# The deformable gather as one stream, its row coordinates all sent by DMA in 8-KB pieces

## The chip, the cores and the metric

The kernel runs on one core of one Trainium2 chip. The metric is the device time of one launch in microseconds, the median of the runs. Everything is float32 at the interfaces; some matmuls read their operands as float32r or bf16.

## The reference, cut to what matters

The network has four layers. The first is a gated selective scan, the second a mixture of experts, the third a bottleneck of three deformable convolutions, the fourth a wide 1x1 mix. The change touches the third layer only: the function `_deform` there, called three times, on 8 images of 256, 64 and 64 channels of 32x32 pixels.

```python
def _deform(x, ow, ob):                      # x: (8, C, 32, 32)
    off = _conv(x, ow, 1) + ob               # two offsets for each channel and pixel
    py = jnp.clip(yy + off[:, :, 0], 0.0, H - 1)
    px = jnp.clip(xx + off[:, :, 1], 0.0, W - 1)
    y0, x0 = floor(py), floor(px); y1, x1 = min(y0 + 1, H - 1), min(x0 + 1, W - 1)
    wy, wx = py - y0, px - x0
    v00, v01, v10, v11 = g(y0, x0), g(y0, x1), g(y1, x0), g(y1, x1)   # g: gather inside the channel
    return v00*(1-wy)*(1-wx) + v01*(1-wy)*wx + v10*wy*(1-wx) + v11*wy*wx
```

Each output pixel of each channel is thus a bilinear sample of that channel's own 32x32 image at a position of its own.

## The kernel before

**The gather without a gather.** The kernel does no indexed access. `build_offsets_1` and `build_middle` write to HBM, for each channel, the image as steps (`dense`: differences of neighbours in both directions), the positions split in a high and a low part (`coords`), and the row positions whole (`whole`). `build_gather` then computes, for 32 rows i and a channel, kw = min(max(py + 1 - i, 0), 1), the same for the columns (vw), and sums dense[i, j] * kw[i] * vw[j] over i and j. The step form of the image makes this the bilinear sample.

**Sets, quads and units.** 128 channels are a set. There are 16 sets in the first gather (g1, 256 channels), 4 in the second (g2) and 4 in the third (g3). A set has 2 halves of 512 pixels (`HALF`) with 8 quads each, so 16 quads; a quad is 16 channels, laid out as 4 groups r of 32 partitions by 4 units c. All three gathers together have 384 quads. Four sets make one turn of a loop (`nc.Fori(0, blocks // SETS)`): g1 has 4 turns, g2 and g3 one each, 6 turns of 64 quads. A turn is a block of its own: its engines start together, all semaphores wait for the end, and nothing of the next turn is loaded before.

**One quad, by engine.** SP (`send_rows`) waits until the row buffer is free (`rows` has SB = 3 slots) and sends, for each r, the row positions of 3 channels (SENT = 3) from `whole` to 32 partitions, each partition the same bytes: 4 DMAs of 3 x 2 KB x 32. VectorE (`relu`) adds 1 - i and takes the maximum with 0 over those 3 units at once, into `kw`. The fourth unit (OWN = 1) comes another way: TensorE spreads its coordinate with a 128x128 selection matmul (`spread_step`, task "k") into a ring of 3 PSUM banks, ScalarE evacuates it. The four column units come by the same ring (tasks "v"), so 5 spread matmuls and 5 evacuations a quad. GpSimd clamps the four `kw` units at 1. TensorE sums over rows (`rows_step`, 16 small 32x32 matmuls into 4 PSUM banks that are not doubled), VectorE multiplies the result by `vw` out of these banks (`weigh`, two instructions of 128x1024), TensorE sums over columns (`fold_step`, 4 matmuls).

**What sets the order.** TensorE takes in turn n: rows_step(n), three spreads, fold_step(n-1), the other spreads. VectorE takes weigh(n) and then relu(n+2). rows_step(n) waits for weigh(n-1), because it writes the banks that weigh reads; weigh(n) waits for rows_step(n). SP issues in program order on one queue: the rows of quad 0, all loads of the first set, the rows of quads 1 and 2, all loads of the other three sets, and only then the rows of quad 3 and on. The loads of a set (`load_set`) are 4 DMAs of 512 KB for `coord` (both directions, high and low: 128 partitions, L1351) and 4 of 128 KB for `img` (L1357), which pick 128-byte pieces out of `dense`. Results go out every 8 quads by one DMA of 256 KB (`store`, L1363).

## Time and profile before

| | |
|---|---|
| median of 3 runs | 5976.52 us (5972.13 to 5980.63) |
| the profiled execution | 5969.8 us, of it the span 5968.1 us |
| TensorE busy | 81% of the span, mean granted clock 0.887 |
| VectorE, ScalarE, GpSimd busy | 60%, 31%, 25% |
| DMA | 558.13 MB in 377577 packets; 37.7% of 16 engines |
| the gathers with the two middle stages between them | about 3610 to 5781 us of the span |
| row positions sent | 1536 DMAs of 192 KB |

The page divides the span into 40 slices. The last 16 of them are this part of the kernel; there DMA stands at 8 and 9 tenths in most slices, and in most slices before at 0 or 1. The shares of the whole span therefore say little about it: the part has to be read by windows. In the rows below, a line of the windows view gives each engine's busy time and, behind PEclk, the granted TensorE clock as a part of 2.4 GHz (0.50 is 1.2 GHz), the mean busy share of the 16 DMA engines (it passes 1 where packets of one engine overlap) and the rate.

### The profile page before, as it was taken

Reading aid. Unit: us, or ns where it says so; the run is one execution under the profiler, and the core shown is the slowest. Engines: PE = TensorE matmul, PEld = TensorE weight load, DVE = VectorE, ACT = ScalarE, POOL = GpSimd, SP = SyncE. Lnnn points to the kernel's source line nnn. Section 1 sums busy time; section 2 is a strip of 40 time slices with the busy share of each in tenths; the row PEclk is TensorE's granted clock in tenths of the full one; section 3 lists DMA queues with packets and bytes.
Section 4 is the critical chain, followed back from the end, with each engine's and each line's share of the span. In section 5 each row is a group of like instructions: output and inputs, shape, how many; then the busy total and the mean of one; then the engine's idle time right before and its main releaser. Section 6 shows DMA issues by size and latency. Waiting matters only on the chain. (4 is left out here: it accounts for less than half of the span.)

```text
span 5968.1 us, 82574 instructions
## 1 busy us (share of the span) xinstructions
PE 4860.9 (81%) x30592; PEld 2689.8 (45%) x30592; DVE 3608.7 (60%) x4317; ACT 1857.1 (31%) x2899; POOL 1478.1 (25%) x1828
## 2 busy tenths in 40 slices
PE   4787887876999799979989994959596983985886
PEld 2333333324777677757767771313131332332222
DVE  6888888875666566652212223848484873863764
ACT  2222222202222122220000003848484751751660
POOL 0222222220000000011101002636363651642540
PEclk7888888867999899989999996979797996997988
DMA  1000000001000000011111119989898968978962
GB/s 30 15 20 17 21 22 21 15 21 65 15 15 8 22 15 15 8 61 74 43 71 74 53 67 193 217 180 218 178 220 181 217 171 183 218 145 143 221 178 91
DMA packets 377577, 558.13 MB, mean 94 GB/s; under 512 B 167464, under 2 KB 169064, under 8 KB 376264
## 3 DMA queue, kind: packets, MB, share of 16 engines
q1 hardware_dynamic: 377160, 552.64, 37.7%
q8 instruction: 253, 4.15, 0.3%
q14 instruction: 164, 1.34, 0.1%
HBM read 439.27 MB, written 113.25 MB: 93 GB/s over the span
## 5 line engine op out<-in xcount | busy, mean ns | idle before, releaser
L1415 POOL TENSOR_SCALAR g_kw<-g_kw 128x512 f32<-128x512 f32 x1536 | 960.8, 650 | 936.7 <-ACT g_kw L1401 637.1
L1401 ACT ACTIVATE g_vw<-ps,l_index 128x512 f32<-128x512 f32 x1536 | 971.0, 686 | 520.4 <-PE ps L1457 520.1
L1434 DVE SCALAR_TENSOR_TENSOR g_prod<-g_vw,ps 128x1024 f32<-128x1024 f32 x768 | 903.3, 1218 | 213.0 <-PE ps L1472 213.0
L1294 PE MATMUL ps<-o_pad,o_ow 128*128 128x512 f32 x3456 | 852.5, 409 | 8.5 <-DVE o_pad L822 7.7
L1457 PE MATMUL ps<-g_coord,l_spread 128*128 128x512 f32 x1920 | 678.5, 452 | 147.6 <-DMA g_coord<-coords 147.4
L1093 PE MATMUL ps<-l_pair,l_w 128*128 128x512 f32 x3072 | 780.3, 403 | 0.0
L1294 PEld LDWEIGHTS ps<-o_pad,o_ow 128*128 128x128 f32 x3456 | 657.3, 191 | 198.0 <-DVE o_pad L822 7.9
L1472 PE MATMUL ps<-g_kw,g_img 32*32 32x512 f32 x12288 | 458.9, 620 | 311.7 <-DVE g_prod L1434 272.5
L1457 PEld LDWEIGHTS ps<-g_coord,l_spread 128*128 128x128 f32 x1920 | 313.1, 194 | 831.1 <-ACT g_vw L1401 615.6
L1093 PEld LDWEIGHTS ps<-l_pair,l_w 128*128 128x128 f32 x3072 | 575.6, 191 | 156.6 <-issue 29.4
L1423 DVE TENSOR_SCALAR g_kw<-g_rows,l_index 128x1536 f32<-128x1536 f32 x384 | 389.8, 1015 | 416.0 <-DMA g_rows<-whole 416.0
L1401 ACT ACTIVATE g_kw<-ps,l_index 128x512 f32<-128x512 f32 x384 | 264.5, 689 | 1098.3 <-PE ps L1457 1081.6
L752 PE MATMUL ps<-l_rows_p,l_sel 72*128 72x512 bf16 x768 | 293.8, 473 | 211.0 <-DVE l_dbx L609 127.2
L1482 PE MATMUL ps<-g_prod,l_fold 128*32 128x512 f32 x3072 | 413.9, 611 | 9.5 <-DVE g_prod L1434 9.5
L1038 DVE TENSOR_TENSOR l_act<-ps,l_act 128x512 f32<-128x512 f32 x256 | 177.0, 691 | 398.0 <-ACT l_act L966 397.5
L428 POOL TENSOR_TENSOR l_acc<-l_acc,l_seen 128x1024 f32<-128x1024 f32 x112 | 283.2, 2528 | 512.9 <-DVE l_seen L619 512.9
L1105 PE MATMUL ps<-l_mixed,l_w 128*128 128x512 f32 x1536 | 401.3, 396 | 3.5 <-DVE l_mixed L822 1.9
L966 ACT ACTIVATE l_act<-ps 128x512 f32<-128x512 f32 x256 | 153.3, 599 | 776.1 <-PE ps L1093 776.1
L130 POOL TENSOR_TENSOR l_moments<-l_moments,l_minus_half 128x2 f32<-128x2 f32 x24 | 16.6, 692 | 1444.2 <-DVE l_moments L99 1444.2
L1105 PEld LDWEIGHTS ps<-l_mixed,l_w 128*128 128x128 f32 x1536 | 287.7, 188 | 79.0 <-issue 7.3
L1472 PEld LDWEIGHTS ps<-g_kw,g_img 32*32 32x32 f32 x12288 | 106.0, 104 | 468.6 <-POOL g_kw L1415 275.6
L1132 DVE SCALAR_TENSOR_TENSOR o_pos<-ps,o_ob,o_grid 128x1024 f32<-128x1024 f32 x32 | 41.1, 1283 | 442.2 <-PE ps L1294 441.9
(247 smaller groups left out, 4911.9 us busy)
## 6 DMA issues: line engine op xcount, KB each, us to landing
g_rows<-whole SPq DMA_DIRECT2D x1536, 192.0 KB, 4.4
g_coord<-coords SPq DMA_DIRECT2D x96, 512.0 KB, 7.2
coords<-o_parts SPq DMA_DIRECT2D x32, 1024.0 KB, 4.0
l_x<-xcur SPq DMA_DIRECT2D x16, 1024.0 KB, 6.5
coords<-o_parts SPq DMA_DIRECT2D x32, 512.0 KB, 5.1
g_img<-dense SPq DMA_DIRECT2D x96, 128.0 KB, 8.6
gathered<-g_res SPq DMA_DIRECT2D x48, 256.0 KB, 4.8
l_xn<-in_x SPq DMA_DIRECT2D x8, 1024.0 KB, 5.0
```

The costliest lines, as they stand in the source:

```text
L428: ins = nc.gpsimd.tensor_tensor(acc[:, h, :], acc[:, h, :], seen[:, i % 2, :], ALU.add)
L752: ins = nc.tensor.matmul(ps[:, lo:lo + HALF], sel[:, q, :], rows_p[:, mine, h, j * HALF:(j + 1) * HALF], start=True, stop=True)
L1093: ins = nc.tensor.matmul(bank(b_ + i % 2), w[:, a, k, e, f * P:(f + 1) * P], pair[:, m % 2, c, k, j * HALF:(j + 1) * HALF], start=(k == 0 ...
L1105: ins = nc.tensor.matmul(bank(5 + c), w2[:, a, f, e, c * P:(c + 1) * P], mixed2[:, i % 3, d, :], start=(e == 0 and f == 0 and r == 0), sto ...
L1294: ins = nc.tensor.matmul(ps[:, lo:lo + HALF], ow[:, a, kk, tap, y, k * P:(k + 1) * P], padded_rows(pad[:, m, c, kk], j, tap), start=(n == ...
L1401: nc.scalar.activation(to, bank(a % RING), ACT.Relu, bias=index[:, 0:1]).then_inc(sem("ring_read"), 1)
L1415: nc.gpsimd.tensor_scalar(part, part, 1.0, 0.0, ALU.min, ALU.max).then_inc(sem("clamped"), 1)
L1423: nc.vector.tensor_scalar(kw[:, q % KB, OWN:4, :].rearrange("p c n -> p (c n)"), rows[:, q % SB].rearrange("p c n -> p (c n)"), index[:, 0 ...
L1434: nc.vector.scalar_tensor_tensor(prod[:, n % PB, 2 * half:2 * half + 2, :].rearrange("p r n -> p (r n)"), vw[:, n % VB, 2 * half:2 * half ...
L1457: nc.tensor.matmul(bank(a % RING), spread[:, int(kind == "v"), h, c, :], coord[:, s, t, j * HALF:(j + 1) * HALF], start=True, stop=True).t ...
L1472: ins = nc.tensor.matmul(ps[c * SIDE:(c + 1) * SIDE, lo:lo + HALF], img[mine, s, g, c, :], kw[mine, n % KB, c, :], start=True, stop=True)
L1482: ins = nc.tensor.matmul(ps[r * SIDE:(r + 1) * SIDE, FOLD_BANK * HALF:(FOLD_BANK + 1) * HALF], fold[:, g, :], prod[:, n % PB, r, :], start ...
```

## The change

The gather becomes one block without a loop over turns: all sets of a gather (16, 4, 4) are unrolled into one stream. SETS is gone; `coord` and `img` have 2 slots and are loaded one set ahead, in the midst of the stream (`load_image` after the rows of quad 7 of the set before, `load_columns` one piece after each of quads 8 to 11). The unit that TensorE spread itself is gone: all four units of a quad are sent (OWN = 0), so 4 spreads and 4 evacuations a quad remain and VectorE's relu covers 128x2048. Only column coordinates are loaded to `coord` (80 partitions of which 64 are loaded, in 4 DMAs of 16 partitions; the other 16 are set to 0 once). `whole` is laid out so that the four channels of a unit group lie side by side: a piece of 8 KB for each partition. The four DMAs of a quad go out in the order r = 0, 2, 1, 3. `dense` is laid out by rows, so that `img` is loaded in 4-KB pieces and stored in 128-byte pieces. `coords` has high and low side by side for each channel.

```diff
-        with nc.Fori(0, blocks // SETS) as turn:          # one block per turn of 4 sets
+        with nc.Block() as block:                         # one block per gather
...
-        coord = st.sb("coord", [P, SETS, 4, N], F32R)
-        img = st.sb("img", [P, SETS, QUADS, 4, SIDE])
-        rows = st.sb("rows", [P, SB, SENT, HALF])         # SENT = 3
+        coord = st.sb("coord", [CROWS, 2, 4, N], F32R)    # CROWS = 80
+        img = st.sb("img", [P, 2, QUADS // 2, 8, SIDE])
+        rows = st.sb("rows", [P, SB, 4, HALF])
...
-            order = [("v", n + 1, 0), ("v", n + 1, 1), ("v", n + 1, 2), ("k", n + 2, 0), ("v", n + 1, 3)]
+            return [(n + 1, c) for c in range(4)] if 0 <= n + 1 < Q else []
...
-                        for r in range(4):
-                            sp.dma_start(rows[r * SIDE:(r + 1) * SIDE, q % SB],
-                                         src[r, OWN:4].partition_broadcast(SIDE)).then_inc(sem(f"rows_sent{q % SB}"), 16)
+                    for r in (0, 2, 1, 3):
+                        lo = r * SIDE + 8 * t + channel_of(h, 0)
+                        sp.dma_start(rows[r * SIDE:(r + 1) * SIDE, q % SB].rearrange("p c n -> p (c n)"),
+                                     whole[s, j, lo:lo + 4].rearrange("q n -> (q n)").partition_broadcast(SIDE))\
+                          .then_inc(sem(f"rows_sent{q % SB}"), 16)
...
+                def load_image(s):
+                    if s >= 2:
+                        sp.wait_ge(sem("rows_summed"), PER_SET * (s - 1))
+                    for r in range(4):
+                        mine = slice(r * SIDE, (r + 1) * SIDE)
+                        sp.dma_start(img[mine, s % 2].rearrange("p t q j -> p (t q j)"),
+                                     dense[s, :, mine, :].rearrange("i q j -> i (q j)")).then_inc(sem(f"img_loaded{s % 2}"), 16)
+                def load_columns(s, r):
+                    sp.dma_start(coord[16 * r:16 * (r + 1), s % 2].bitcast(F32),
+                                 coords[s, 1, r * SIDE:(r + 1) * SIDE].rearrange("(t q) s n -> (q s) t n", t=4))\
+                      .then_inc(sem(f"coord_loaded{s % 2}"), 16)
...
+                send_rows(0)
+                for r in range(4):
+                    load_columns(0, r)
+                load_image(0)
+                send_rows(1)
+                send_rows(2)
+                for q in range(SB, Q):
+                    send_rows(q)
+                    s, part = divmod(q, PER_SET)          # PER_SET = 16
+                    if s + 1 < sets:
+                        if part == 7:
+                            load_image(s + 1)
+                        if 8 <= part < 12:
+                            load_columns(s + 1, part - 8)
+                    if q % QUADS == SB + 2 and q >= QUADS:
+                        store(q // QUADS - 1)
...
-                        nc.vector.tensor_scalar(kw[:, q % KB, OWN:4, :].rearrange("p c n -> p (c n)"),
+                    nc.vector.tensor_scalar(kw[:, q % KB, :, :].rearrange("p c n -> p (c n)"),
...
-        dense = dram("dense", (B * C, N))
+        dense = dram("dense", (B * C // P, SIDE, P, SIDE))
-        coords = dram("coords", (B * C // P, 2, 2, P, N))
-        whole = dram("whole", (B * C // P, P, N))
+        coords = dram("coords", (B * C // P, 2, P, 2, N))
+        whole = dram("whole", (B * C // P, NH, P, HALF))
```

New is `channel_of(h, c)`, which returns 4 * h + c. The stores of `dense`, `coords` and `whole` in `build_offsets_1` and `build_middle` follow the new layouts; in `build_offsets_1` the store of an image's `dense` is 2 DMAs in place of one. The selection matrices `spread` and `fold` are built for the new order of channels.

## Rows read from the trace of the kernel before

**Rows 1.** Windows view, a steady stretch of the gather (busy us, count; PEclk; DMA share; GB/s).
```profile
4050.00:4150.00 100.00, 97.25 (x1202) 31.84 (x1202) 86.14 (x79) 83.69 (x136) 65.69 (x105) 1.00 0.91 215
```
**Rows 2.** Timeline of one steady quad: start, us, engine, line, operation, count, idle before.
```profile
4103.30 1.01 DVE L1423 TENSOR_SCALAR g_kw<-g_rows,l_index 128x1536 f32<-128x1536 f32 x1
4103.52 1.15 PE L1472 MATMUL ps<-g_kw,g_img 32*32 32x512 f32 x32
4104.84 2.35 DVE L1434 SCALAR_TENSOR_TENSOR g_prod<-g_vw,ps 128x1024 f32<-128x1024 f32 x2 [0.53 <-PE ps L1472]
4106.50 0.74 PE L1457 MATMUL ps<-g_coord,l_spread 128*128 128x512 f32 x2
4107.34 1.15 PE L1472 MATMUL ps<-g_kw,g_img 32*32 32x512 f32 x32
```
**Rows 3.** Instructions of L1434 in five of six turns: min/median/max ns, first and last start.
```profile
L1434 DVE SCALAR_TENSOR_TENSOR g_prod<-g_vw,ps x128: 1212/1216/1223, 3633.6 to 3914.4; 128x1024 f32<-128x1024 f32 x128
L1434 DVE SCALAR_TENSOR_TENSOR g_prod<-g_vw,ps x128: 1214/1216/1223, 3950.9 to 4232.0; 128x1024 f32<-128x1024 f32 x128
...
L1434 DVE SCALAR_TENSOR_TENSOR g_prod<-g_vw,ps x128: 1212/1215/1223, 4585.5 to 4866.3; 128x1024 f32<-128x1024 f32 x128
L1434 DVE SCALAR_TENSOR_TENSOR g_prod<-g_vw,ps x128: 1212/1216/1223, 5027.8 to 5310.3; 128x1024 f32<-128x1024 f32 x128
L1434 DVE SCALAR_TENSOR_TENSOR g_prod<-g_vw,ps x128: 1214/1216/1223, 5497.1 to 5778.5; 128x1024 f32<-128x1024 f32 x128
```
**Rows 4.** Waits from 3590 to 3720 us: total us, times, longest.
```profile
DVE g_kw L1423 <- DMA g_rows<-whole: 60.6, 5, 37.1
```
**Rows 5.** Windows view: row DMAs in a backlog; `coord` loads alone; loads over 128 partitions.
```profile
3676.00:3692.00 16.00, 10.75 (x124) 3.53 (x125) 11.11 (x11) 6.22 (x10) 7.57 (x13) 0.71 1.06 216
3654.00:3661.00 7.00, 0.00 (x0) 0.00 (x0) 0.00 (x0) 0.00 (x0) 0.00 (x0) 0.50 1.03 250
4945.00:4952.00 7.00, 5.03 (x16) 1.60 (x16) 0.00 (x0) 3.10 (x4) 0.00 (x0) 0.77 1.02 414
```
**Rows 6.** Windows view: stores from partitions 0-63; the same with partitions 64-127 among them.
```profile
4906.00:4908.00 2.00, 2.00 (x13) 1.34 (x13) 1.97 (x2) 0.00 (x0) 2.00 (x1) 1.00 0.91 193
4909.00:4913.00 4.00, 4.00 (x21) 1.90 (x18) 3.90 (x5) 1.53 (x2) 2.48 (x1) 1.00 0.87 249
```
**Rows 7.** DMA issues of the whole run: count, KB each, median us from issue to landing.
```profile
g_rows<-whole SPq DMA_DIRECT2D x1536, 192.0 KB, 4.4
g_img<-dense SPq DMA_DIRECT2D x96, 128.0 KB, 8.6
dense<-o_step SPq DMA_DIRECT2D x16, 256.0 KB, 5.1
```
**Rows 8.** Instructions of L1423, L136 and L1415, whole run: min/median/max ns.
```profile
L1423 DVE TENSOR_SCALAR g_kw<-g_rows,l_index x384: 1012/1015/1022, 3615.8 to 5772.0; 128x1536 f32<-128x1536 f32 x192
L136 DVE TENSOR_SCALAR l_xn<-l_x,l_moments x32: 805/811/815, 1401.7 to 5952.5; 128x1024 f32<-128x1024 f32 x32
L1415 POOL TENSOR_SCALAR g_kw<-g_kw x1536: 604/612/823, 3619.8 to 5774.6; 128x512 f32<-128x512 f32 x192
```
**Rows 9.** Timeline at a turn's start: the loop once, at the low clock.
```profile
3633.56 2.35 DVE L1434 SCALAR_TENSOR_TENSOR g_prod<-g_vw,ps 128x1024 f32<-128x1024 f32 x2
3636.05 2.02 PE L1472 MATMUL ps<-g_kw,g_img 32*32 32x512 f32 x32 [8.85 <-DVE g_prod L1434]
3638.24 2.35 DVE L1434 SCALAR_TENSOR_TENSOR g_prod<-g_vw,ps 128x1024 f32<-128x1024 f32 x2 [1.02 <-PE ps L1472]
```

**Rows 10.** Windows view, a turn's stall (as rows 1).
```profile
3634.00:3676.00 42.00, 9.54 (x90) 2.82 (x90) 5.28 (x5) 6.22 (x10) 4.44 (x8) 0.58 1.10 210
```

More of the change, by code:

```diff
@@ L32 @@
 QUADS = P // (UNITS * 4)
-SETS = 4
+CROWS = 80
 IMGS = 4
@@ L1231, in _ @@
                     for m in range(IMGS):
-                        sp.wait_ge(sem(f"stored{m}"), 16)
+                        sp.wait_ge(sem(f"stored{m}"), 16 * KC)
                 @block.gpsimd
@@ L1298, in build_offsets_1, with channel_of, build_gather @@
             st.clear()
-def build_gather(nc, ps, consts, dense, coords, whole, gathered, blocks, tag):
+def channel_of(h, c):
+    return 4 * h + c
+def build_gather(nc, ps, consts, dense, coords, whole, gathered, sets, tag):
     with ExitStack() as ctx:
@@ L1315, in build_gather @@
         res = st.sb("res", [P, 2, HALF])
-        rows = st.sb("rows", [P, SB, SENT, HALF])
-        quads = [(s, j, g) for s in range(SETS) for j in range(NH) for g in range(QUADS)]
-        Q = len(quads)
+        rows = st.sb("rows", [P, SB, 4, HALF])
+        quads = [(s, j, g) for s in range(sets) for j in range(NH) for g in range(QUADS)]
+        Q, PER_SET = len(quads), NH * QUADS
         bank = lambda i: ps[:, i * HALF:(i + 1) * HALF]
@@ L1323, in turn_tasks @@
         def turn_tasks(n):
-            order = [("v", n + 1, 0), ("v", n + 1, 1), ("v", n + 1, 2), ("k", n + 2, 0), ("v", n + 1, 3)]
-            return [t for t in order if 0 <= t[1] < Q]
+            return [(n + 1, c) for c in range(4)] if 0 <= n + 1 < Q else []
         for n in range(-2, Q):
@@ L1500, in batch_norm_setup @@
+        st.clear()
 def batch_norm_setup(nc, dve, link, sem, cols, out, count):
@@ L1539, in load_constants @@
     c = {
-        "spread": st.sb("spread", [P, 2, 2, 4, P], F32R), "fold": st.sb("fold", [P, QUADS, BLK]),
+        "spread": st.sb("spread", [CROWS, 2, 5, P], F32R), "fold": st.sb("fold", [P, QUADS, BLK]),
         "index": st.sb("index", [P, 1]),
@@ L1551, in load_constants @@
     with ExitStack() as own:
-        spread_f = own.enter_context(nc.sbuf_tensor("spread_f", [P, 2, 2, 4, P], F32))
+        spread_f = own.enter_context(nc.sbuf_tensor("spread_f", [CROWS, 2, 5, P], F32))
         ow_f = {n: own.enter_context(nc.sbuf_tensor(f"ow_f{n}", [P, 6, P], F32)) for n in (2, 3)}
@@ L1586, in _ @@
                 dve.wait_ge(sem("loaded"), 16 * len(loads))
-                link(nc.vector.tensor_copy(c["spread"][:, :, :, :, :], spread_f[:, :, :, :, :]))
+                link(nc.vector.tensor_copy(c["spread"][:, :, :, :], spread_f[:, :, :, :]))
                 for n in (2, 3):
@@ L1637, in _ @@
                         sp.wait_ge(sem("steps_ready"), m + 1)
-                        sp.dma_start(dense[bass.ds(b * CM, CM), :], step[:, m, :]).then_inc(sem("stored"), 16)
+                        part = slice(m % 2 * CM, (m % 2 + 1) * CM)
+                        sp.dma_start(dense[bass.ds(turn * (PASS // 2) + m // 2, 1), :, part, :].rearrange("a i p j -> (a p) i j"),
+                                     step[:, m, :].rearrange("p (i j) -> p i j", j=SIDE)).then_inc(sem("stored"), 16)
                         sp.wait_ge(sem("coords_ready"), m + 1)
@@ L1641, in _ @@
                             half = slice(m % 2 * CM, (m % 2 + 1) * CM)
-                            sp.dma_start(coords[bass.ds(turn * (PASS // 2) + m // 2, 1), y, :, half, :]
-                                         .rearrange("a s p n -> (a p) s n"),
+                            sp.dma_start(coords[bass.ds(turn * (PASS // 2) + m // 2, 1), y, half, :, :]
+                                         .rearrange("a p s n -> (a p) s n"),
                                          co.stored(slice(y * CM, (y + 1) * CM), m)).then_inc(sem(f"coords_stored{m}"), 16)
-                        sp.dma_start(whole[bass.ds(turn * (PASS // 2) + m // 2, 1), half, :].rearrange("a p n -> (a p) n"),
-                                     co.pos[0:CM, m % 2, :]).then_inc(sem(f"coords_stored{m}"), 16)
+                        sp.dma_start(whole[bass.ds(turn * (PASS // 2) + m // 2, 1), :, half, :].rearrange("a j p n -> (a p) j n"),
+                                     co.pos[0:CM, m % 2, :].rearrange("p (j n) -> p j n", j=NH)).then_inc(sem(f"coords_stored{m}"), 16)
                     for m in range(PASS):
@@ L1902, in constants @@
         sel_experts[e::E, e, :] = 1
-    spread = np.zeros((2, 2, UNITS, 2, 4, 2, 2, 4, P), np.float32)
+    cols = np.zeros((UNITS, 8, 2, 2, 5, P), np.float32)
+    rest = np.zeros((16, 2, 5, P), np.float32)
+    fold = np.zeros((P, QUADS, BLK), np.float32)
     for h in range(2):
-        for n in range(4):
-            for q in range(4):
-                spread[0, :, q, h, n, 0, h, n, q * SIDE:(q + 1) * SIDE] = 1
-                spread[1, :, n, h, q, 1, h, n, q * SIDE:(q + 1) * SIDE] = 1
-    spread = spread.reshape(P, 2, 2, 4, P)
-    fold = np.zeros((P, QUADS, BLK), np.float32)
-    for g in range(QUADS):
-        fold[p, g, 4 * g + p // SIDE] = 1
+        for q in range(4):
+            mine = slice(q * SIDE, (q + 1) * SIDE)
+            for n in range(4):
+                cols[n, channel_of(h, q), :, h, n, mine] = 1
+            for t in range(QUADS // 2):
+                fold[mine, 2 * t + h, 8 * t + channel_of(h, q)] = 1
+    spread = np.concatenate([cols.reshape(CM, 2, 5, P), rest])
     return {
```

278 lines of the change are left out of this document (124 added, 154 removed).

## The prediction

> **What bounds the kernel now.** I read first the page's slices, to see that the gathers are the only part of the kernel where DMA works at 8 or 9 tenths, then windows of it. In a steady stretch TensorE is busy 97.25 of 100 us at the full clock of 2.4 GHz, VectorE 86.14, and DMA has a share of 0.91 at 215 GB/s [rows 1]. Three things are near their end at once, so the next view is the timeline of one quad [rows 2]. The row matmuls begin at 4103.52 and again at 4107.34, a period of 3.82 us. Between them lies a closed loop: row matmuls start 4103.52, weigh starts 4104.84 (1.32 later), both weighs end 4107.19 (2.35), the next row matmuls start 0.15 after. 1.32 + 2.35 + 0.15 = 3.82. The last spread ends at 4107.24, 0.10 before the row matmuls, so TensorE's own work is the shorter by a hair; VectorE idles 0.53 before the weigh. The loop of rows_step and weigh sets the pace.
>
> Second, the turns. Within a turn first and last weigh are 280.8 to 282.5 us apart [rows 3]; 63 periods and one half-quad step are 63 x 3.817 + 1.1 = 241.6, so about 40 us are lost in each turn, in one piece: VectorE's relu waits up to 37.1 us for the row positions of quad 3 [rows 4], which stand in SP's queue behind the loads of three sets. Between the turns of g1 another 36 us pass (3914.4 to 3950.9, and two more like it) [rows 3]. From first to last weigh g1 takes 3633.6 to 4866.3 = 1232.7, g2 282.5, g3 281.4 [rows 3], together 1796.6 us. That is the sum against which the change is set.
>
> **The stream and the loads of a set.** One stream removes the 6 stalls of 40 and the 3 gaps of 36: some 348 us, if the rest kept its pace. Left would be 381 gaps between quads (255 + 63 + 63) at 3.82, or 1455 us. Before the first weigh nothing is gained: it comes after relu(1), hence after rows 0, the whole first set and rows 1, in both kernels; 2 MB + 0.5 MB + 1.6 MB before, 1 + 0.5 + 2.1 MB after.
>
> **One spread and one evacuation less.** Worth nothing: the loop above has neither in it, and TensorE's slack grows from 0.10 to some 0.5 us a quad.
>
> **The relu grows** from 1536 to 2048 elements a partition. 1024 took 811 ns and 1536 took 1015 [rows 8], so 0.40 ns an element and 1.22 us; in proportion it would be 1.35. The 0.20 to 0.34 more lie in VectorE's 0.53 us of idle time [rows 2]. GpSimd's four clamps are 4 x 0.612 = 2.45 us [rows 8]; even strung to the relu they make 3.80. Cost 0; without that cover 0.3 us a quad at most.
>
> **The row positions.** A quad now sends 4 x 262 = 1049 KB in place of 786 KB. At the pace of 3.82 us this needs 275 GB/s, and the loads of the next set come on top. What can the queue give? When it has a backlog, right after the stall, row DMAs run at 216 GB/s with a DMA share above 1 [rows 5]: already 786 KB take 3.64 us. Loads over all 128 partitions run at 414 [rows 5], so it is not HBM and not the 16 engines, but something that a DMA to 32 partitions meets. The 8-KB pieces alone thus don't help; what may help is the order 0, 2, 1, 3. Two rows bear on it. Stores from partitions 0-63 ran at 193 GB/s, and as soon as a DMA from 64-127 followed, at 249 [rows 6]. The `coord` loads of the kernel before, alone on the queue, 512 KB each in 4-KB pieces to all partitions, ran at 250 [rows 5]; why not at 414 the trace doesn't say. Nothing shows the order 0, 2, 1, 3 itself, so the bounds are 216 (no gain) and 414 (both halves at once). I take 250, because two different rows in which the halves are mixed agree on it: 1049 / 250 = 4.19 us a quad, 381 x 4.19 = 1598 us.
>
> The Trainium skill, page "SBUF — State Buffer", section "Door 1: The DMA port swizzle", says that partitions 0 to 31 reach 8 of 16 DMA ports, all even, and that 64 to 127 are on the odd ones; by this a quarter DMA has half the rate, and the trace agrees (216 against 414). The same page, under "Can I just issue two DMAs to hit both halves?", speaks against the order 0, 2, 1, 3: two DMAs on the two halves gave 6% more than one. The trace shows more for stores (193 to 249) and nothing for these loads.
>
> **Loads of the next set, now within the stream.** Column pieces: 21 sets (24 less the 3 first ones) x 4 DMAs of 262 KB to only 16 partitions. Bounds: at 250 GB/s 1.05 us each; at a quarter of 414, since a quarter DMA had half, 2.5 us. I take 2.5: 84 x 2.5 = 210 us (88 at the low end). Image: 84 x 131 KB at 216 = 0.61, 51 us. Result stores: 48 x 0.63 (262 KB at 414) = 30 us. Together 291 us, 169 at the low end. All of it shares SP's one queue with the rows, and once DMA sets the pace none of it is hidden.
>
> **Stages around.** `dense` is written in 128-byte pieces. In `build_offsets_1` matmuls cover it: 0. In the middle stages the store of 256 KB, now 5.1 us to land [rows 7], comes before the last coordinates of each of 4 turns: taken +1.3 us each, 5 in all; 0 to 20 as bounds, from the 128-byte image loads of half the size, 8.6 us [rows 7].
>
> By the Trainium skill, page "DMA: Bandwidth & Descriptors", section "Specifications", pieces under 512 bytes cost a read and a write; no row here shows that for a store.
>
> **Sum.** 1598 + 291 = 1889 for the three gathers, 4.96 us a quad, against 1796.6: +92. With the middle stages +97: the profiled execution of 5969.8 becomes 6067. The median before lies 6.7 above its profiled execution, so 6074 us. So DMA takes the place of the loop as the bound, and gives back more than the stalls were worth. TensorE will idle and its clock may fall from 2.4 GHz towards 1.2, as it does in the stalls of before (0.58 on average [rows 10]); there the loop took 4.68 us (3633.56 to 3638.24) [rows 9], still under 4.96.
>
> **The rivals.**
> (a) **The halves overlap in full.** Then the rows take 1049 / 414 = 2.53 us and with the other loads 3.3, under the loop's 3.82. The gathers take 1455 us, -342, and the median becomes 5640. For it: the queue can give 414 GB/s over all partitions [rows 5], and a DMA's rate rises as soon as one to the other half stands beside it [rows 6]. Against it: the mixed rows stop at 250.
> (b) **They overlap in part**, at 300 GB/s: 1049 / 300 = 3.50 us, 1332 + 291 = 1623, -174 + 5: 5808. The point that decides between faster and slower is (1796.6 - 291 - 5) / 381 = 3.94 us a quad, 266 GB/s. Against it only that no row reaches 266 in a stretch of quarters; for it that the halves change at every DMA here, and at every second one in the backlog of before.
> (c) **No overlap at all**, on the slower side of my forecast: 216 GB/s, 4.86 us a quad, 1850 + 291 = 2141, +344 + 5: 6326. For it: in the backlog rows two of four changes of DMA already cross from one half to the other, and 216 is all they give [rows 5].
> (d) The loads of the next set cost only their low bound: 1598 + 169 = 1767, -30 + 5: 5952, a form of my forecast that ends on the faster side.
>
> **How the numbers follow.** My forecast 0.42, (a) 0.14, (b) 0.18, (c) 0.20, (d) 0.06. The forecast's own range is 5950 to 6330, from (d) to (c). For 8 in 10 it must reach over (b): 5740 to 6330, leaving out (a) and a little above (c). A measurement of this kernel can tell 0.2%, 12 us. Faster by more: (a), (b), half of (d), 0.36; slower by more: (c) and nearly all of the forecast, 0.58; 0.06 within.
>
> **What would show it.** In the profile after: the DMA share near 1 through the whole gather and its rate (216, 250 or 300 and more); relu waiting for rows in nearly every quad, where it waited 5 times at a turn's start; the period from one weigh to the next, 4.96 on average, about 4.2 in quads without set loads and longer in quads 7 to 11; no stall of 40 us; TensorE at about 70% busy or at a lower clock. The relu at 1.22 us. Wrong would be: a period of 3.82 with relu seldom waiting (then (a)), or relu above 1.4 us and VectorE without idle time (then it is the bound, not DMA).

## The result, and the profile after

The changed kernel takes 6031.81 us (median of 4 runs, 6022.99 to 6043.72); the kernel before took 5978.13 beside it. The ratio is 1.0093, interval 1.0071 to 1.0114: it is 0.9% slower. 6074 had been predicted, in a range of 5740 to 6330. The profiled execution of after is 6037.97 us, its span 6036.3, mean granted clock 0.856 (before 0.887).

The page of after: its slices (40 over the span; PEclk and DMA in tenths), then the rows of the costliest groups, answering to [rows 1] and [rows 8].

```profile
PEclk7888888867999899989999986888877786897877
DMA  0000000001000000012122129999999978978972
...
L1427 DVE TENSOR_SCALAR g_kw<-g_rows,l_index 128x2048 f32<-128x2048 f32 x384 | 493.5, 1285 | 409.6 <-DMA g_rows<-whole 408.5
L1438 DVE SCALAR_TENSOR_TENSOR g_prod<-g_vw,ps 128x1024 f32<-128x1024 f32 x768 | 902.1, 1216 | 126.9 <-PE ps L1478 126.0
```

DMA stands at 9 tenths through the whole of g1 and drops only between gathers. VectorE's relu (now L1427, 1285 ns) has 408.5 us of idle time ahead of it, all of it put down to the row positions. Before, the relu waited for them 60.6 us at the start of a turn [rows 4], and in all 416.0 us in 30 waits; now it waits 408.5 us in 202. The sum has hardly changed: what was a few long stalls is now spread over the whole gather.

The weighs of the three gathers: min/median/max ns, first and last start.

```profile
L1438 DVE SCALAR_TENSOR_TENSOR g_prod<-g_vw,ps x512: 1208/1214/1223, 3639.5 to 4897.6; 128x1024 f32<-128x1024 f32 x171
L1438 DVE SCALAR_TENSOR_TENSOR g_prod<-g_vw,ps x128: 1211/1215/1223, 5060.0 to 5356.5; 128x1024 f32<-128x1024 f32 x128
L1438 DVE SCALAR_TENSOR_TENSOR g_prod<-g_vw,ps x128: 1211/1215/1223, 5542.5 to 5843.5; 128x1024 f32<-128x1024 f32 x128
```

From first to last weigh g1 takes 1258.1, g2 296.5 and g3 301.0 us, together 1855.6, where it was 1796.6 [rows 3]: +59.0. The rest of the profiled +68.2 is +5.9 before the first weigh, +0.9 and -0.8 between the gathers and +3.2 at the end. So 59 of the 68 us, and the whole gain that didn't come, lie inside the gathers. The 5.9 us before the first weigh are within the scatter of that point: it lies at 3634.3 us in e3 and at 3647.5 in e2, whose code before it differs from that of after at most in where the columns land.

Where inside, the relu's starts over one set and a little more show (timeline of VectorE, line L1427; start, us, and in brackets the idle time before):

```profile
4281.87 1.28 DVE L1427 TENSOR_SCALAR g_kw<-g_rows,l_index 128x2048 f32<-128x2048 f32 x1
4285.69 1.28 DVE L1427 TENSOR_SCALAR g_kw<-g_rows,l_index 128x2048 f32<-128x2048 f32 x1
4289.50 1.28 DVE L1427 TENSOR_SCALAR g_kw<-g_rows,l_index 128x2048 f32<-128x2048 f32 x1
4294.21 1.29 DVE L1427 TENSOR_SCALAR g_kw<-g_rows,l_index 128x2048 f32<-128x2048 f32 x1 [0.81 <-DMA g_rows<-whole]
4298.54 1.28 DVE L1427 TENSOR_SCALAR g_kw<-g_rows,l_index 128x2048 f32<-128x2048 f32 x1 [0.78 <-DMA g_rows<-whole]
4306.53 1.29 DVE L1427 TENSOR_SCALAR g_kw<-g_rows,l_index 128x2048 f32<-128x2048 f32 x1 [4.45 <-DMA g_rows<-whole]
4313.42 1.29 DVE L1427 TENSOR_SCALAR g_kw<-g_rows,l_index 128x2048 f32<-128x2048 f32 x1 [3.33 <-DMA g_rows<-whole]
4321.54 1.28 DVE L1427 TENSOR_SCALAR g_kw<-g_rows,l_index 128x2048 f32<-128x2048 f32 x1 [4.58 <-DMA g_rows<-whole]
4328.73 1.29 DVE L1427 TENSOR_SCALAR g_kw<-g_rows,l_index 128x2048 f32<-128x2048 f32 x1 [3.65 <-DMA g_rows<-whole]
4334.58 1.29 DVE L1427 TENSOR_SCALAR g_kw<-g_rows,l_index 128x2048 f32<-128x2048 f32 x1 [2.30 <-DMA g_rows<-whole]
4338.25 1.29 DVE L1427 TENSOR_SCALAR g_kw<-g_rows,l_index 128x2048 f32<-128x2048 f32 x1
4343.09 1.28 DVE L1427 TENSOR_SCALAR g_kw<-g_rows,l_index 128x2048 f32<-128x2048 f32 x1
4346.91 1.28 DVE L1427 TENSOR_SCALAR g_kw<-g_rows,l_index 128x2048 f32<-128x2048 f32 x1
```

Two regimes are to be seen. At 4281.87, 4285.69 and 4289.50 the period is 3.82, the old loop. At the loads of the next set it is 6.9 to 8.1, each time with 3.3 to 4.6 us of waiting for rows. Now the mean over g1 of the gap from one weigh to the next, by the place of the second one in its set (quads 0 to 15, as in the code). It is 3.8 to 4.1 us for quads 0 to 4, 6.6 to 6.8 for quads 7 to 10, 5.1 to 5.6 for quads 11 to 13 and 3.8 at quad 15. The mean of all is 4.93 us.

Windows of after: g1 but for its ends, then an unloaded stretch, a loaded one, and two right behind it (busy us of the engines; PEclk; DMA share; GB/s).

```profile
3660.00:4890.00 1230.00, 1064.51 (x11001) 310.51 (x11000) 887.92 (x750) 647.77 (x1032) 584.29 (x999) 0.80 1.01 240
4275.00:4291.00 16.00, 14.62 (x209) 4.61 (x178) 14.71 (x13) 10.60 (x17) 9.50 (x17) 1.00 1.02 241
4300.00:4330.00 30.00, 22.02 (x185) 5.93 (x184) 13.99 (x13) 12.04 (x20) 9.27 (x16) 0.66 1.03 183
4330.00:4340.00 10.00, 9.00 (x81) 2.18 (x77) 7.12 (x7) 3.22 (x5) 5.06 (x9) 0.50 1.03 270
4341.00:4372.00 31.00, 28.23 (x355) 8.93 (x353) 29.14 (x25) 21.06 (x34) 17.86 (x31) 1.00 1.03 272
```

The DMA share is 1.01 to 1.03 in all of these windows, but what is moved in that time differs: 183 GB/s where set loads are in the queue, 241 to 272 where it carries rows, a store of results and at most the first bytes of the next images. And TensorE's clock is at the lower level (1.2 GHz, 0.50) in the first quads behind the waits.

### The profile page after: what moved, and what is told of

Its sections match the earlier page's. It is cut to its first block and busy times, and to the rows that moved or that the text cites. A ratio compares the mean times of both kernels' runs of the same rounds, so it can differ in the third digit from the quotient of the medians.

```text
span 6036.3 us, 78036 instructions
## 1 busy us (share of the span) xinstructions
PE 5025.5 (83%) x30208; PEld 2699.4 (45%) x30208; DVE 3730.3 (62%) x4320; ACT 1632.4 (27%) x2515; POOL 1416.4 (23%) x1828
## 3 DMA queue, kind: packets, MB, share of 16 engines
q14 instruction: 126, 1.03, 0.1%
## 5 line engine op out<-in xcount | busy, mean ns | idle before, releaser
L1417 POOL TENSOR_SCALAR g_kw<-g_kw 128x512 f32<-128x512 f32 x1536 | 899.0, 612 | 1061.0 <-DVE g_kw L1427 1061.0
L1463 PE MATMUL ps<-g_coord,l_spread 80*128 80x512 f32 x1536 | 668.8, 523 | 113.8 <-DMA g_coord<-coords 113.8
L1478 PE MATMUL ps<-g_kw,g_img 32*32 32x512 f32 x12288 | 543.4, 738 | 256.2 <-POOL g_kw L1417 198.0
L1427 DVE TENSOR_SCALAR g_kw<-g_rows,l_index 128x2048 f32<-128x2048 f32 x384 | 493.5, 1285 | 409.6 <-DMA g_rows<-whole 408.5
L1463 PEld LDWEIGHTS ps<-g_coord,l_spread 80*128 80x128 f32 x1536 | 307.0, 222 | 956.1 <-ACT g_vw L1406 602.8
L1488 PE MATMUL ps<-g_prod,l_fold 128*32 128x512 f32 x3072 | 497.1, 725 | 4.7 <-DVE g_prod L1438 4.7
L613 DVE TENSOR_TENSOR_SCAN l_states<-ps,l_dbx 128x1024 f32<-128x1024 f32 x128 | 293.2, 2290 | 23.5 <-PE ps L752 19.8
```

What stands on the lines that cost most here:

```text
L613: nc.vector.tensor_tensor_scan(states[:, i % 2, :], ps[:, 0:2 * HALF], dbx[:, i % 2, :], 0.0, ALU.mult, ALU.add).then_inc(sem("da_used"), 1)
L1417: nc.gpsimd.tensor_scalar(part, part, 1.0, 0.0, ALU.min, ALU.max).then_inc(sem("clamped"), 1)
L1427: nc.vector.tensor_scalar(kw[:, q % KB, :, :].rearrange("p c n -> p (c n)"), rows[:, q % SB].rearrange("p c n -> p (c n)"), index[:, 0:1], ...
L1463: nc.tensor.matmul(bank(a % RING), spread[:, h, c, :], coord[:, s % 2, t, j * HALF:(j + 1) * HALF], start=True, stop=True).then_inc(sem("r ...
L1478: ins = nc.tensor.matmul(ps[c * SIDE:(c + 1) * SIDE, lo:lo + HALF], img[mine, s % 2, g // 2, channel_of(g % 2, c), :], kw[mine, n % KB, c, ...
L1488: ins = nc.tensor.matmul(ps[r * SIDE:(r + 1) * SIDE, FOLD_BANK * HALF:(FOLD_BANK + 1) * HALF], fold[:, g, :], prod[:, n % PB, r, :], start ...
```

## Experiments

Each kernel is the changed one with one edit, or builds on an experiment named. The sum of the three gathers (first to last weigh of each, read as above, in the one profiled execution) is the number to compare; beside it stand the median and the ratio to the kernel before, which ran on the same chip. e2 and e7 leave out a part of the data and serve as measurements of time only.

| kernel | gathers, us | median, us | ratio to before (interval) |
|---|---|---|---|
| before | 1796.6 | 5978.13 | 1 |
| after | 1855.6 | 6031.81 | 1.0093 (1.0071 to 1.0114) |
| e1_order | 1999.9 | 6154.28 | 1.0273 (1.0233 to 1.0313) |
| e2_rows_only | 1608.0 | 5790.25 | 0.9691 (0.9659 to 0.9722) |
| e3_columns_apart | 1752.4 | 5919.35 | 0.9913 (0.9886 to 0.9940) |
| e4_2kb_pieces | 1887.0 | 6060.64 | 1.0145 (1.0100 to 1.0191) |
| e5_three_sent | 1729.0 | 5912.53 | 0.9882 (0.9859 to 0.9905) |
| e7_three_of_four | 1500.8 | 5660.34 | 0.9472 (0.9456 to 0.9488) |
| e9_one_dma | 3949.9 | 8178.38 | 1.3689 (1.3667 to 1.3712) |
| e10_own_apart | 1647.1 | 5822.72 | 0.9753 (0.9736 to 0.9771) |
| e11_loads_spread | 1537.6 | 5710.75 | 0.9563 (0.9546 to 0.9581) |
| e12_spread_order | 1646.2 | 5840.39 | 0.9791 (0.9758 to 0.9825) |

**e1_order: the order of the four row DMAs undone.**

```diff
-                    for r in (0, 2, 1, 3):
+                    for r in (0, 1, 2, 3):
```

> The changed kernel with the four row DMAs of a quad in the order r = 0, 1, 2, 3. My theory: a DMA to 32 partitions gets half of the queue's rate, and changing the half at every DMA (0, 2, 1, 3) lets one overlap a little with the next; with half of these changes gone the rows fall from about 250 towards 216 GB/s. The three gathers, 1856 us in the changed kernel, become 1950 to 2110 us and the kernel 6120 to 6280 us. Rival: the order does nothing, and the 250 GB/s come from the larger pieces: 6032 us within 15.

Measured: 6154.28 us, the gathers 144 us longer. Window of e1 over g1:

```profile
3660.00:5000.00 1340.00, 1101.39 (x10999) 315.54 (x10999) 889.31 (x751) 646.57 (x1029) 586.48 (x1000) 0.78 1.01 220
```

Both numbers lie in the expected ranges. It is 220 GB/s at the same DMA share of 1.01, where after has 240. The unloaded quads 0 to 4 now take 4.1 to 4.4 us in place of 3.8 to 4.1. So the order is worth 144 us / 381 = 0.38 us a quad, and it is the part of the change that keeps it within 1% of before. That it works by the change of halves is the reading that the expectation had; no other order that changes halves at every DMA was run. The 220 GB/s contain the set loads and are not to be set beside the 216 of [rows 5], which are rows alone.

**e2_rows_only: the set loads taken out of the stream.** From the third set of each gather on, `coord` and `img` are not loaded, and the old contents are used.

```diff
-                    if s + 1 < sets:
+                    if s + 1 < 2:
...
-                        pe.wait_ge(sem(f"coord_loaded{s % 2}"), 64 * (s // 2 + 1))
+                        pe.wait_ge(sem(f"coord_loaded{s % 2}"), 64)
...
-                        pe.wait_ge(sem(f"img_loaded{s % 2}"), 64 * (s // 2 + 1))
+                        pe.wait_ge(sem(f"img_loaded{s % 2}"), 64)
```

> The changed kernel without the loads of column coordinates and images of the sets from the third on (their data stay those of the first two; only the time is of interest). It measures what the row positions need by themselves. My theory of the prediction, rows at 250 GB/s: 4.19 us a quad, gathers 1597 us, kernel about 5775 us. Rival one, rows fit under the loop of 3.82 us: 1455 us, kernel about 5632 us. Rival two, rows at 216 GB/s: 1850 us, kernel about 6025 us.

Measured: 5790.25 us (5775 expected), gathers 1608.0 (1597 expected). Window over its g1, and its longest waits in 3660 to 4600:

```profile
3660.00:4690.00 1030.00, 895.04 (x11085) 277.25 (x11077) 895.73 (x755) 652.42 (x1038) 589.38 (x1004) 0.97 1.01 266
```
```profile
DVE g_kw L1427 <- DMA g_rows<-whole: 95.0, 149, 4.3
DVE g_prod L1438 <- PE ps L1478: 28.0, 78, 2.6
```

18 of 21 set loads are out, and the gathers are 247.6 us shorter: 13.8 us a set. Rows alone still don't run at the loop's pace: there are 149 short waits, and taking off 3 sets at 13.8 and the stores at 30, 1536 us / 381 = 4.03 us a quad are left, 260 GB/s. The 4.03 is a difference and takes two things as given: that the 3 sets left cost as much each as the 18 taken out, and that the stores cost 30. This splits the loss in its two terms. Rows: 381 x (4.03 - 3.82) = 80 us over the loop. Set loads: 290 us. With 30 of stores that is 400 us: the 342 that the gathers had over 381 bare periods of the loop (1796.6 - 1455), and 58 more.

**e3_columns_apart: the 16 partitions of a column piece four apart.** The same bytes, the same number of DMAs; the selection matrix is built for the new places.

```diff
-                    sp.dma_start(coord[16 * r:16 * (r + 1), s % 2].bitcast(F32),
+                    sp.dma_start(coord[r:CM:4, s % 2].bitcast(F32),
...
-    cols = np.zeros((UNITS, 8, 2, 2, 5, P), np.float32)
+    cols = np.zeros((8, 2, UNITS, 2, 5, P), np.float32)
...
-                cols[n, channel_of(h, q), :, h, n, mine] = 1
+                cols[channel_of(h, q), :, n, h, n, mine] = 1
```

> The changed kernel with the 16 partitions of each column DMA four apart (r, r + 4, ..., r + 60) in place of side by side, and the selection matrix to match. Bytes, pieces and number of DMAs are the same. My theory: a column DMA is slow (2.5 us for 262 KB) because its 16 adjacent partitions reach a quarter of what 128 reach; spread over 64 partitions it should take 1.2 us, 84 x 1.25 = 105 us less: about 5927 us. Rival: its pace is set by the number of pieces or by its place in the queue, not by where it lands: 6032 us within 15.

Measured: 5919.35 us (8 runs), 112 under after and faster than before. Window over g1:

```profile
3660.00:4800.00 1140.00, 990.24 (x10905) 294.97 (x10901) 879.18 (x742) 640.45 (x1020) 578.59 (x989) 0.86 1.02 257
```

That is what was expected (5927). 257 GB/s against 240, at a share of 1.02. The gathers are 103 us shorter: spread over 84 DMAs, 1.23 us each. Quads 7 to 10 of a set take 5.6 to 5.8 us in place of 6.6 to 6.8. Nothing of the transfers but the partitions on which the bytes land is different, so the rate of a DMA here depends on which partitions it reaches. A part of the 1.23 us may be indirect: the quads that are slow at a low clock without waiting for rows (counted further below) cost 38 us in place of 55.

The Trainium skill, page "SBUF — State Buffer", section "Door 1: The DMA port swizzle", gives each DMA port of SBUF to four neighbouring partitions (and to the same four 32 further on). By its table 16 adjacent partitions reach 4 of 16 ports and 16 of them four apart reach 8. The runs agree in direction, with 1.23 us saved a DMA.

**e4_2kb_pieces: row positions in pieces of 2 KB again.** Each row of the buffer is padded, so that a partition gets four pieces of 2 KB in place of one of 8.

```diff
-        rows = st.sb("rows", [P, SB, 4, HALF])
+        rows = st.sb("rows", [P, SB, 4, HALF + 16])
...
-                        sp.dma_start(rows[r * SIDE:(r + 1) * SIDE, q % SB].rearrange("p c n -> p (c n)"),
-                                     whole[s, j, lo:lo + 4].rearrange("q n -> (q n)").partition_broadcast(SIDE))\
+                        sp.dma_start(rows[r * SIDE:(r + 1) * SIDE, q % SB, :, 0:HALF],
+                                     whole[s, j, lo:lo + 4].partition_broadcast(SIDE))\
```

> The changed kernel with each partition's row positions sent as four pieces of 2 KB in place of one of 8 KB (a gap of 64 bytes behind each unit in the row buffer). My theory: the size of the pieces matters little, since the rate is that of the partitions reached: under 1.5% more, 6032 to 6110 us. Rival: the 8-KB pieces are what lifted the rows from 216 to 250 GB/s, then the gathers go to about 2110 us and the kernel to 6280 us.

Measured: 6060.64 us (6042.89 to 6096.66), as the theory had it, gathers +31 us, 0.08 us a quad. The large pieces are worth half a per cent (29 us), not much above the scatter of this kernel's runs; the order (122 us) and the placement of the columns (112 us) are each worth about four times as much.

**e5_three_sent: the stream, but with TensorE spreading one of four units again.** 768 KB of rows a quad, e3's columns, and 4 DMAs of 64 KB a set for the own unit's coordinates, each to 4 adjacent partitions. Core of the edit:

```diff
+            order = [(n + 1, 0), (n + 1, 1), (n + 1, 2), (n + 2, 4), (n + 1, 3)]
...
-                                     whole[s, j, lo:lo + 4].rearrange("q n -> (q n)").partition_broadcast(SIDE))\
+                                     whole[s, j, lo + 1:lo + 4].rearrange("q n -> (q n)").partition_broadcast(SIDE))\
...
+                def load_own(s, part):
+                    h, low = divmod(part, 2)
+                    sp.dma_start(coord[CM + 4 * part:CM + 4 * (part + 1), s % 2].bitcast(F32),
+                                 coords[s, 0].rearrange("(r t m) s n -> m s r t n", r=4, t=4)[channel_of(h, 0), low])\
+                      .then_inc(sem(f"coord_loaded{s % 2}"), 16)
```

> One stream, spread columns as in e3_columns_apart, but only three units of a quad sent by DMA (pieces of 6 KB, 786 KB a quad) and the fourth spread by TensorE as in the kernel before (its coordinates in 4 more DMAs of 64 KB a set). My theory: the changed kernel loses its gain only because DMA passes the loop's 3.82 us. At 250 to 261 GB/s three units need 3.0 to 3.15 us, with the loads of a set some 3.7, so the loop sets the pace again: gathers 1460 to 1500 us, kernel 5640 to 5700 us. Rival: the loads of a set stall the stream whatever the rows need (they did so by 9 us a set in e3_columns_apart): gathers 1455 + 24 x 9, kernel about 5850 us.

Measured: 5912.53 us, a miss by more than 200. Window over g1, then its waits of VectorE from 3660 to 4650:

```profile
3660.00:4800.00 1140.00, 1065.47 (x11141) 333.20 (x11155) 812.81 (x744) 784.42 (x1270) 611.46 (x990) 0.85 0.86 203
```
```profile
DVE g_prod L1455 <- PE ps L1493: 171.8, 172, 3.3
DVE g_kw L1444 <- DMA g_rows<-whole: 117.2, 40, 4.5
```

In quads 3 to 8 of a set the period is 3.82 with five spreads. The fifth spread therefore costs nothing there; the loss sits in quads 9 to 15, at 4.6 to 6.9 us, with some in quads 0 to 2 (4.0 to 4.4), and it has two names: rows that are late (117.2 us in 40 waits) and row matmuls that are late (171.8 us). Two things were new in those quads, the own unit's loads and the spread at a low clock. e7 and e10 take them apart.

**e7_three_of_four: three units sent, nothing in place of the fourth.** e3 with a quarter of the row data left out: unit 0 of the row buffer is constant, everything else is computed.

```diff
-                        sp.dma_start(rows[r * SIDE:(r + 1) * SIDE, q % SB].rearrange("p c n -> p (c n)"),
-                                     whole[s, j, lo:lo + 4].rearrange("q n -> (q n)").partition_broadcast(SIDE))\
+                        sp.dma_start(rows[r * SIDE:(r + 1) * SIDE, q % SB, 1:4].rearrange("p c n -> p (c n)"),
+                                     whole[s, j, lo + 1:lo + 4].rearrange("q n -> (q n)").partition_broadcast(SIDE))\
```

> e3_columns_apart with three units of a quad sent but all four computed on (the first unit of the row buffer is set to 0 once, so a quarter of the row data is missing; only the time is of interest). Against e5_three_sent it prices the spread matmul and evacuation that the change took out: my prediction put them at nothing. Theory: within 12 us of e5_three_sent, 5640 to 5700. Rival: the fourth spread costs its 0.35 to 0.45 us a quad on TensorE: e5_three_sent is 130 to 170 us slower than this one.

Measured: 5660.34 us. The level is the expected one, and near the 5640 of rival (a), but the comparison for which the run was made is a miss: it was to lie within 12 us of e5, by the rival 130 to 170 under it, and it lies 252 under it. Window over g1:

```profile
3660.00:4630.00 970.00, 865.39 (x10896) 273.27 (x10880) 880.18 (x745) 641.79 (x1023) 580.77 (x992) 0.99 0.95 234
```

The loop is the bound again: the median gap is 3.817, clock 0.99, DMA share below 1. Against e3 (1752.4) the missing quarter of the rows is worth 252 us. Against e5 it is 228 in the gathers (1729.0 - 1500.8), and this is the price of the own unit there. The run bounds it but doesn't tell its spread from its loads.

**e10_own_apart: e5 with the own unit's 4 partitions of a DMA four apart.**

The selection matrix is built to match (not shown).

```diff
-                    sp.dma_start(coord[CM + 4 * part:CM + 4 * (part + 1), s % 2].bitcast(F32),
+                    sp.dma_start(coord[CM + part:CROWS:4, s % 2].bitcast(F32),
```

> e5_three_sent with the four partitions of each DMA of own-unit coordinates four apart in place of side by side (selection matrix to match); nothing else. Theory: e5_three_sent lost 250 us against e7_three_of_four because a DMA of 64 KB to 4 adjacent partitions reaches 1 of 16 parts of what 128 partitions reach: 414 / 16 = 26 GB/s, 2.5 us each, 84 of them 210 us, on only the engines that carry it, and all rows behind it wait. Apart they reach four such parts: 0.6 us. Kernel 5665 to 5730 us. Rival: the loss is that such a DMA runs on 4 of 16 engines, wherever it lands: 5880 to 5920 us.

Measured: 5822.72 us, between the two expectations: 90 of the 250 us lay in the placement. 84 DMAs of just 64 KB, 1.0 us each (82 us in the gathers), of which some 20 us come from quads of low clock that are fewer by it. What is left is seen in a timeline behind a load, and in a window of it:

```profile
4249.96 2.35 DVE L1455 SCALAR_TENSOR_TENSOR g_prod<-g_vw,ps 128x1024 f32<-128x1024 f32 x2 [3.28 <-PE ps L1493]
...
4254.30 2.01 PE L1493 MATMUL ps<-g_kw,g_img 32*32 32x512 f32 x32
...
4256.50 2.35 DVE L1455 SCALAR_TENSOR_TENSOR g_prod<-g_vw,ps 128x1024 f32<-128x1024 f32 x2 [3.25 <-PE ps L1493]
```
```profile
4249.00:4269.00 20.00, 20.00 (x163) 5.83 (x147) 11.51 (x11) 10.70 (x18) 8.57 (x15) 0.62 0.46 122
```

The period is 6.54 us with TensorE busy 20.00 of 20 us and DMA at 0.46: nothing waits for DMA. At 1.2 GHz TensorE's own work of a quad with five spreads is the longest thing in it. So one late load costs twice, once as a wait and once more in the quads after it, while the clock is still low.

**e11_loads_spread: e10 with the set's loads spread over nine quads.**

```diff
-                        if part == 7:
-                            load_image(s + 1)
-                        if 8 <= part < 12:
-                            load_columns(s + 1, part - 8)
-                            load_own(s + 1, part - 8)
+                        if 5 <= part < 9:
+                            load_image(s + 1, [part - 5])
+                        if part in (7, 9, 11, 13):
+                            load_columns(s + 1, (part - 7) // 2)
+                        if part in (6, 8, 10, 12):
+                            load_own(s + 1, (part - 6) // 2)
```

> e10_own_apart with the loads of the next set spread thinner over the stream: one image DMA after each of the quads 5 to 8, column DMAs after 7, 9, 11 and 13, own-unit DMAs after 6, 8, 10 and 12. Theory: on average DMA has room under the loop (some 3.6 of 3.82 us), stalls come only where loads stand close together; spread, the loop sets the pace nearly everywhere: 5630 to 5660 us, 20 to 60 under e10_own_apart. Rival: the three row buffers already even this out: within 12 us of e10_own_apart.

Measured: 5710.75 us (5706.54 to 5728.48): 112 under e10, more than expected, though the level of 5630 to 5660 was too low. It computes everything, and it is the fastest complete kernel: 4.4% under before, 5.3% under after. Window over g1 and its waits from 3660 to 4650:

```profile
3660.00:4650.00 990.00, 927.16 (x11214) 303.71 (x11216) 822.86 (x748) 789.24 (x1277) 626.38 (x999) 1.00 0.95 234
```
```profile
DVE g_prod L1456 <- PE ps L1494: 96.8, 186, 0.7
DVE g_kw L1445 <- DMA g_rows<-whole: 70.1, 68, 2.5
```

No byte less is moved than in e10; the clock is 1.00 in place of 0.91, the longest wait for rows 2.5 us in place of 3.8, and that for matmuls 0.7 in place of 3.3. The largest mean gap in a set is 4.5, where it was 6.0. Counted over the three gathers as explained further below, quads that are slow at a low clock without waiting for rows cost 23 us over the loop in place of 98, and quads that wait for rows 57 in place of 91: most of the gain is the clock.

**e12_spread_order: e11 with the rows in the order 0, 1, 2, 3.**

```diff
-                    for r in (0, 2, 1, 3):
+                    for r in (0, 1, 2, 3):
```

> e11_loads_spread with the row DMAs in the order r = 0, 1, 2, 3. Theory: the rows then need 3.5 to 3.65 us a quad, with the set loads about 4.1, over the loop: 5700 to 5790 us. Rival: with three units sent there is room enough and the order no longer matters: within 12 us of e11_loads_spread.

Measured: 5840.39 us, 130 over e11 and 50 above the expected range. The order matters as much as in e1 (+122), though e11 leaves DMA some slack (0.95). An order that is 8% slower by e1's windows (220 against 240) would use that slack up; this fits and isn't separately shown. By the count used for e11 the quads that wait for rows cost 139 us in place of 57, and those slow at a low clock 49 in place of 23.

**e9_one_dma: the rows of a quad in one DMA of 1 MB to all 128 partitions**, the source with its four groups outermost; e3's columns.

```diff
+                    src = whole[s, j].rearrange("(r m) n -> r m n", r=4)[:, m0:m0 + 4].rearrange("r q n -> r (q n)")
+                    sp.dma_start(rows[:, q % SB].rearrange("p c n -> p (c n)"),
+                                 src.unsqueeze(1).to_broadcast([4, SIDE, 4 * HALF])).then_inc(sem(f"rows_sent{q % SB}"), 16)
```

> e3_columns_apart with a quad's row positions in one DMA of 1 MB over all 128 partitions in place of four of 256 KB over 32 each (same bytes, same 8-KB pieces). Theory A, the partitions reached set the rate: all 128 at once give 414 GB/s, 2.5 us a quad, the loop sets the pace, kernel 5650 to 5720 us. Theory B, such a DMA with a source of four blocks goes like the coord loads of the kernel before, 250 GB/s: 4.19 us a quad, no gain, 5919 us within 40. Rival C: the source's outermost size of 4 leaves it with 4 of 16 engines: about 104 GB/s, 10 us a quad, kernel 8000 us or more.

Measured: 8178.38 us, 37% slower. A window of 1000 us within its g1:

```profile
4000.00:5000.00 1000.00, 582.76 (x4221) 152.66 (x4213) 340.53 (x288) 247.12 (x394) 224.67 (x384) 0.51 0.29 114
```

A DMA share of 0.29 and 114 GB/s, while the relu waits for rows in all 384 quads. The number is that of rival C (about 104 GB/s, 8000 us or more), which had 4 of the 16 engines at work; the window gives only the mean share of the 16, not which of them were busy. The 414 GB/s of [rows 5] can't be had for rows by writing them as one transfer in this form.

## Why the prediction was right, and where it was off

The mechanism was right: DMA took the place of the loop as the bound and gave back more than the stalls were worth. How near the number came owes something to luck, as the terms below show.

**Bound of before, stalls and gaps: right.** No stall of 40 us is left. In quads with rows in time the period is 3.82, the old loop, as the timeline above shows. The prediction looked for about 4.2 in quads without set loads and for a relu that waits in nearly every quad; the runs show 3.8 to 4.1, and the relu waits in 202 of 384. What the stream removes (348) is borne out by e7: with rows and loads under the loop's pace the gathers take 1500.8 us, near the 1455 that the prediction gave them.

**Relu, spread and evacuation.** The relu takes 1.285 us (1.22 to 1.35 predicted), inside VectorE's idle time: in the loop of after 0.27 us of it are left, from 0.53 [rows 2]. Timeline of after:

```profile
4287.23 2.35 DVE L1438 SCALAR_TENSOR_TENSOR g_prod<-g_vw,ps 128x1024 f32<-128x1024 f32 x2 [0.27 <-PE ps L1478]
4289.50 1.28 DVE L1427 TENSOR_SCALAR g_kw<-g_rows,l_index 128x2048 f32<-128x2048 f32 x1
4289.73 1.15 PE L1478 MATMUL ps<-g_kw,g_img 32*32 32x512 f32 x32 [0.34 <-DVE g_prod L1438]
```

That the missing spread is worth nothing holds at 2.4 GHz (e5, quads 3 to 8). At 1.2 GHz it doesn't: a quad takes 6.54 us with five spreads (e10) and 6.11 with four (rows below), 0.43 us less.

**Rows: 4.19 us a quad, 4.03 by the difference in e2.** The 250 GB/s taken from [rows 5, 6] were 260. The term was 1598 and is 1536, 62 too high. This is the step that decided between the forecast and its rivals; the turning point of 266 GB/s was missed by 2%. The order 0, 2, 1, 3 lifts the rate, as argued, but it explains only a part of the step from 216 [rows 5]. Without it the gathers give back 144 us (e1); if set loads and stores cost the same 320 there, the rows of e1 need (1999.9 - 320) / 381 = 4.41 us, 238 GB/s (an estimate). From 216 to 238 is then something else; e4 gives the larger pieces 0.08 us a quad, some 5 GB/s, and the rest stays open.

**Set loads and stores: 291, by the runs 320.** With the stores left at 30, which no run took out, a set's loads are 290 / 21 = 13.8 us, not 12.4. The 2.5 us for a column DMA to 16 partitions was a quarter of 414. e3 bounds it from below: four apart it is 1.23 us faster. If it then takes 1.0 us (262 KB at 260 GB/s), it took 2.2 (an estimate). Then the images cost (13.8 - 8.9) / 4 = 1.2 us each in place of 0.61; no run took these apart, so that split is argued and not shown.

**The sum.** Predicted were 1889 for the gathers, measured are 1855.6. The terms from the runs, 1536 + 290 + 30 = 1856, don't confirm this by themselves: rows and set loads were both taken from the difference of after and e2, so their sum gives after back by construction. What e2 adds is the split. The errors of -62 and +29 partly cancel, and the forecast was 42 us too high. That is the luck in the number.

**The clock: it fell as foreseen, and the statement on its cost was wrong.** The prediction has the loop at a low clock at 4.68 [rows 9], below the period of 4.96, hence no cost. But [rows 9] is the first quad of a turn, in which TensorE had idled 8.85 us before its row matmuls and had neither a fold nor more than the start of its spreads between the two weighs. In full a quad at 1.2 GHz takes 6.11 us. Timeline of after behind loaded quads, and windows of two such quads and of a third in another set:

```profile
3865.21 2.35 DVE L1438 SCALAR_TENSOR_TENSOR g_prod<-g_vw,ps 128x1024 f32<-128x1024 f32 x2 [2.57 <-PE ps L1478]
...
3869.12 2.01 PE L1478 MATMUL ps<-g_kw,g_img 32*32 32x512 f32 x32
...
3871.32 1.22 DVE L1438 SCALAR_TENSOR_TENSOR g_prod<-g_vw,ps 128x1024 f32<-128x1024 f32 x1 [2.56 <-PE ps L1478]
```
```profile
3859.09:3865.21 6.12, 6.12 (x45) 1.61 (x46) 3.55 (x4) 2.53 (x4) 4.55 (x8) 0.50 1.01 293
3865.21:3871.32 6.11, 6.11 (x45) 1.60 (x46) 3.55 (x4) 2.53 (x4) 2.34 (x4) 0.50 0.80 213
4814.53:4820.65 6.12, 6.12 (x45) 1.61 (x46) 3.55 (x4) 2.53 (x4) 3.12 (x6) 0.50 1.02 260
```

TensorE is busy the whole 6.11 us, so at the low clock its own work sets the pace and no longer the loop of rows_step and weigh. The second mistake was to compare with the mean period. The quads of low clock are the ones right after the loaded ones, where the rows come back in time; there TensorE, not DMA, is the longer.

How much is it? Count a quad as slow when the gap from its weigh to the next is over 3.82 us by more than 0.15. Over the gathers of after, 34 quads are slow without a wait for rows between the two weighs, 55 us over the loop together; 198 gaps have such a wait, 341 us together. Yet most of the 55 us cost nothing here: in 28 of the 34 the DMA share is 0.96 or more, as in the first and third window, so DMA runs on and the row buffers fill in the meantime. In the other 6 it falls to between 0.72 and 0.87, as in the second window; set against a share of 1.02, the DMA time lost in the 34 is about 8 us (an estimate). So "no cost" came out nearly true for another reason than the one given. In e5 and e10 the same count gives 119 and 98 us; there the DMA share over g1 is only 0.86 and 0.88, and the cost is real.

**The middle stages: too dear, and made good by chance.** Between the gathers, where the prediction put 5 us, the difference is +0.1 (+0.9 and -0.8). All that lies outside the gathers is +9.3, but it stands before the first weigh (+5.9, within the scatter named above) and behind the last (+3.2), where the prediction had nothing.

**The rivals.** (a) would have needed 414 GB/s for halves that alternate; the runs stop at 260 for quarters. (c) didn't come true even without the new order: e1 took 6154 us where (c) priced 6326, with rows at some 238 GB/s by the estimate above, not 216. (b) and (d) failed on the same two terms, at 260 GB/s and 13.8 us a set.

**What stays open.** Why `coord` loads over all 128 partitions ran at 250 before and not at 414 [rows 5]. Why rows in the order 0, 1, 2, 3 run at some 238 in the stream and ran at 216 in the backlog of before. And why the halves in turn give 260 and not twice 216: none of the runs separates a limit of the queue from one of the partitions reached.

## What to carry to other kernels

Before moving work from an engine that isn't the bound to DMA, divide the bytes by the rate of that very form of transfer (which partitions, in which order), and add what else the queue must carry in the same stretch: here 1049 KB a quad at 260 GB/s is 4.03 us against a loop of 3.82, and the loads took the rest. Try small loads on partitions four apart, let neighbouring DMAs alternate between the halves (the changed kernel did so already), and spread the loads of the next set over many iterations: the fourth unit back on TensorE, the loads four apart and their spreading turned a loss of 0.9% into a gain of 4.4%. Judge what an idle spell costs by a full iteration at the low clock, in the iterations behind it, and not by the mean period; and look whether DMA runs on in them.

## What the runs showed of the hardware that was not expected

- The cost of a DMA goes by the partitions that it reaches, down to small ones: 16 partitions four apart in place of adjacent save 1.23 us on 262 KB (e3, where it had been expected), 4 partitions four apart in place of adjacent save 1.0 us on 64 KB (e5 against e10), both with what the clock gives back.
- Quarter DMAs in the order 0, 2, 1, 3 give 240 GB/s over g1, in the order 0, 1, 2, 3 220 (e1), both with a DMA share of 1.01; some 260 for rows alone (by difference, e2). The Trainium skill, page "SBUF — State Buffer", section "Can I just issue two DMAs to hit both halves?", has 6% for two DMAs on the two halves against one; the step from 220 to 240 that the order alone made in this stream is 9%.
- A DMA whose source has 4 as its outermost size left the DMA share at 0.29 and the rate at 114 GB/s, though it fed 128 partitions (e9).
- A clock that has fallen in waits for DMA stays low for some quads although TensorE is then busy all the time (20.00 of 20 us at 0.62, e10), and at 0.50 a quad takes 6.54 us with five spreads (e10) and 6.11 with four (after) in place of 3.82.
